# Transformer tower on one core: one softmax bound per head, auxiliary pieces on even quads, a rewritten preparation

## The reference

```python
patches = 8x8 patches of x                                  # 1024 tokens of 64 values
h = patches @ W.T + b + pos_embed                           # [1024, 64]
y = layernorm(h)
q, k, v = y@Wq + bq, y@Wk + bk, y@Wv + bv                   # 8 heads of 8
scores = q.k / sqrt(8) + col_bias[head, key]                # 1024 x 1024 per head
h = h + softmax(scores) @ v @ Wo + bo
z = layernorm(h)
h = h + z + sum over the 2 best of 8 experts of weight_e * (gelu(z@w1[e] + b1[e]) @ w2[e] + b2[e])
```

## Time and profile before

| | us |
|---|---|
| median of 3 runs | 1176.74 |
| the profiled execution | 1175.44 |
| its span, first to last instruction | 1173.6 |
| TensorE busy in it | 1105.3 (94%) |
| ScalarE busy | 1030.7 (88%) |
| VectorE busy | 671.2 (57%) |
| first to last exp of the attention stage | 56.18 to 1011.50 |

### The profile page before, as it was taken

How to read it: one execution, slowest core, us unless ns; L and a number is a source line. 1 busy time by engine, 2 the same in 40 slices (tenths; PEclk the granted TensorE clock), 3 DMA queues, 4 the chain that set the end, 5 groups by cost and what they waited for, 6 DMA issues and landing times. The chain is left out here.

```text
span 1173.6 us, 21907 instructions
## 1 busy us (share of the span) xinstructions
PE 1105.3 (94%) x7938; PEld 326.1 (28%) x7938; DVE 671.2 (57%) x1899; ACT 1030.7 (88%) x1127; POOL 131.8 (11%) x137
## 2 busy tenths in 40 slices
PE   3399999999999999999999999999999999899998
PEld 3122222222222222222222222222222222233332
DVE  9542756565656555565656565656565624367665
ACT  0199999999999999999999999999999999754553
POOL 4302201010101010101010101010101100000000
PEclk8589999999999999999999999999999999999999
DMA  2421323232323232323232323222222220022332
GB/s 52 111 74 39 85 53 82 53 83 53 83 53 84 53 83 53 83 49 87 49 88 49 86 50 73 63 68 67 62 67 55 72 61 10 16 63 66 84 75 50
DMA packets 63041, 75.93 MB, mean 65 GB/s; under 512 B 26338, under 2 KB 31458, under 8 KB 62906
## 3 DMA queue, kind: packets, MB, share of 16 engines
q1 hardware_dynamic: 60076, 73.01, 25.1%
q10 hardware_dynamic: 2350, 1.10, 0.4%
q0 software_dynamic: 480, 0.06, 0.1%
HBM read 37.54 MB, written 36.49 MB: 63 GB/s over the span
## 5 line engine op out<-in xcount | busy, mean ns | idle before, releaser
L1247 ACT ACTIVATE probs<-psum 128x1024 f32<-128x1024 f32 x1024 | 946.5, 1144 | 13.2 <-PE psum L1446 10.9
L1462 PE MATMUL psum<-probs,VA 128*32 128x512 f32 x4096 | 547.0, 606 | 5.3 <-DVE oT L1315 0.9
L1446 PE MATMUL psum<-QA,KA 54*128 54x512 bf16 x2048 | 331.7, 385 | 20.0 <-ACTq L1266 9.1
L1446 PEld LDWEIGHTS psum<-QA,KA 54*128 54x128 bf16 x2048 | 75.0, 93 | 491.5 <-ACT probs L1247 448.3
L1315 DVE STREAM_TRANSPOSE oT<-psum 128x512 f32<-128x512 f32 x64 | 45.9, 717 | 143.3 <-PE psum L1462 143.3
L1462 PEld LDWEIGHTS psum<-probs,VA 128*32 128x32 f32 x4096 | 82.1, 108 | 144.6 <-issue 86.1
L1282 ACT ACTIVATE probs<-psum,b 128x1024 f32<-128x1024 f32 x64 | 67.9, 1111 | 53.6 <-PE psum L1515 53.5
L1393 DVE TENSOR_TENSOR probs<-probs,psum 128x1024 f32<-128x1024 f32 x64 | 78.2, 1221 | 51.6 <-PE psum L1525 30.4
L484 DVE TENSOR_SCALAR qk<-psum,b_qk,scale_qk 128x512 f32<-128x512 f32 x32 | 25.8, 810 | 134.4 <-PE psum L673 134.4
L1515 PE MATMUL psum<-m_x,w 64*128 64x512 f32 x256 | 60.5, 591 | 1.5 <-ACT probs L1282 1.5
L1539 PE MATMUL psum<-probs,w 128*64 128x512 f32 x256 | 60.9, 598 | 0.0
(11 more groups left out here) (175 smaller groups left out, 830.9 us busy)
## 6 DMA issues: line engine op xcount, KB each, us to landing
QA<-q_parts_d SPq DMA_DIRECT2D x64, 192.0 KB
KA<-k_parts_d SPq DMA_DIRECT2D x64, 192.0 KB
q_parts_d<-qk_parts SPq DMA_DIRECT2D x31, 192.0 KB, 2.5
k_parts_d<-qk_parts SPq DMA_DIRECT2D x31, 192.0 KB, 2.7
xT<-in_xT SPq DMA_DIRECT2D x16, 256.0 KB, 2.6
x_d<-x2T SPq DMA_DIRECT2D x16, 256.0 KB, 2.1
m_x<-x_d SPq DMA_DIRECT2D x16, 256.0 KB, 2.7
out_h<-result SPq DMA_DIRECT2D x16, 256.0 KB, 3.2
```

Of the source, the lines that this page charges most:

```text
L1247: nc.scalar.activation(probs[:, k % PROB_BUFS, :], score_buf(buf_of(k)), ACT.Exp).then_inc(exped, 1)
L1446: last = pe.matmul(score_buf(buf_of(k))[:, (g % 2) * BANK:(g % 2 + 1) * BANK], KA[rows_of(h, SCORE_ROWS), h // 2, jt * P:(jt + 1) * P], QA ...
L1462: last = pe.matmul(o_acc[32 * g:32 * g + 32, :], VA[:, jt, h, :], probs[:, k % PROB_BUFS, (g % 2) * BANK:(g % 2 + 1) * BANK], start=(jt == ...
```

## The change

- **One bound per head.** The per-query shift goes, with `shift_of`, `sq`'s copy, the store to DRAM and its load. Instead `sq` clips the root `rq` at 32 and spreads it over a diagonal; a new piece `bound` (in place of `flag`) multiplies it with ones, so that all partitions have the 8 roots, and VectorE reduces them to `lift`, one negative bound per pair of heads. The exp takes it as its bias. The shift rows of QA are filled with zeros by `load_shift`. The column bias has its own maximum subtracted once.
- **Even quads.** The pieces get other slots, and so do scale, centre, lead, normalise, weigh and the router's exp.
- **GpSimd's order.** In an image `prep_rstd` now comes ahead of `copy_v(0)`; in the preparation `prep_rq(0)` comes ahead of `prep_rstd(1)`.
- **Preparation.** One-hots with three instructions over pairs of edges; VA zeroed by ScalarE; the fills of `ones3` and `zeros3` after the one-hots; bias rows moved from SBUF to SBUF in six transfers, three on each of two queues; the exp table used early; 8 warm-up matmuls at the end of TensorE's part; the second half of q and k parts stored by SP at the start of the attention stage.

```diff
-AUX_SLOTS = {0: ("qk0", 0), 1: ("qk0", 1), 2: ("qk1", 0), 4: ("qk1", 1), 6: ("out_proj", 0), 7: ("out_proj", 1),
-             10: ("sq", 0), 13: ("post_t", 0), 16: ("router", 0), 18: ("router", 1), 19: ("flag", 0), 20: ("v", 0),
-             21: ("v", 1), 23: ("embed", 0), 24: ("embed", 1), 26: ("combine_t", 0), 29: ("norm_t", 0)}
+AUX_SLOTS = {0: ("qk0", 0), 2: ("qk0", 1), 4: ("qk1", 0), 6: ("qk1", 1), 8: ("out_proj", 0), 10: ("out_proj", 1),
+             12: ("sq", 0), 14: ("post_t", 0), 15: ("bound", 0), 16: ("router", 0), 18: ("router", 1), 20: ("embed", 0),
+             22: ("embed", 1), 24: ("v", 0), 26: ("v", 1), 28: ("combine_t", 0), 30: ("norm_t", 0)}
-CENTRE_SLOT, SCALE_SLOT, LEAD_SLOT, NORM_SLOT = 7, 9, 25, 27
-ROUTER_EXP_BLOCK = 38
+CENTRE_SLOT, SCALE_SLOT, LEAD_SLOT, NORM_SLOT = 10, 12, 23, 26
+ROUTER_EXP_BLOCK = 40
-COMBINE_SLOT, WEIGH_SLOT = 20, 22
+COMBINE_SLOT, WEIGH_SLOT = 20, 25
-RQ_LIMIT = 31.0
+RQ_LIMIT, RQ_CLIP = 31.0, 32.0
+WARM_MATMULS = 8
...
                 elif step == "sq":
-                    v.tensor_copy(sq[:, :], bank)
                     v.reduce_max(sq_max[:, :], bank, AX.X).then_inc(free, 1)
                     v.wait_ge(free, freed)
                     alone(v)
                     square_bounds(link)
-                    shift_of(bp, link, close)
-                elif step == "flag":
-                    v.tensor_scalar(flags[0:1, ds(bp, 1)], bank[0:1, 0:1], 1.0, None,
-                                    ALU.min).then_inc(free, 1)
+                    v.wait_ge(rq_ready, bp + 1)
+                    link(v.tensor_scalar(rq_clipped[:, :], rq[:, :], RQ_CLIP, None, ALU.min))
+                    close()
+                    v.tensor_scalar(rq_diag[:, :], ident[0:H, 0:H], rq_clipped[:, 0:1], None,
+                                    ALU.mult).then_inc(rq_spread, 1)
+                elif step == "bound":
+                    v.tensor_reduce(rq_top[:, :], bank[0:1, 0:H], AX.X, ALU.max)
+                    v.tensor_reduce(lift[:, bp % 2, :], bank[:, 0:H].rearrange("p (j t) -> p j t", t=2), AX.X, ALU.max,
+                                    negate=True).then_inc(free, 1)
...
-                elif step == "flag":
-                    pe.wait_ge(excess_ready, n + 1)
+                elif step == "bound":
+                    pe.wait_ge(rq_spread, n + 1)
                     alone(pe)
-                    last = pe.matmul(aux[0:1, 0:1], excess[:, :], ones8[:, :], start=True, stop=True)
+                    last = pe.matmul(aux[:, 0:H], ones8[:, :], rq_diag[:, :], start=True, stop=True)
...
+            def place_bias(eng, par):
+                eng.wait_ge(bparts_ready, 1)
+                for a in range(PARTS):
+                    r = HALF_ROWS * par + BIAS_ROW + a
+                    eng.dma_start(KA[r:r + 1, :, :].rearrange("o h (c p) -> o (h c) p", p=P),
+                                  bparts[32 * par:32 * par + 32, a, :]).then_inc(bparts_moved, 16)
...
-                    for n in range(32):
-                        v.tensor_scalar(hot_b[:, n, :], node_bf[:, :], float(n), exp_bits[:, 0:1].bitcast(F32),
-                                        ALU.is_equal, ALU.mult)
-                    for n in range(32):
-                        last = v.tensor_scalar(hot_a[:, n, :], node_af[:, :], float(n), None, ALU.is_equal)
-                    last.then_inc(hot_ready, 1)
+                    link(v.tensor_tensor(hot_b[:, :, :, :], nodes_b, each, ALU.is_equal))
+                    v.tensor_scalar(hot_b[:, :, :, :], hot_b[:, :, :, :], exp_bits[:, 0:1].bitcast(F32), None, ALU.mult)
+                    v.tensor_tensor(hot_a[:, :, :, :], nodes_a, each, ALU.is_equal).then_inc(hot_ready, 1)
+                    v.memset(ones3[:, :], 1.0).then_inc(ones_ready, 1)
+                    v.memset(zeros3[:, :], 0.0).then_inc(ones_ready, 1)
...
+                    for n in range(WARM_MATMULS):
+                        pe.matmul(first_bank["qk1"], ident_bf[:, :],
+                                  hot_b[:, 0:8, :, :].rearrange("p m b t -> p (m b t)"), start=True, stop=True)
...
-                    nc.scalar.activation(probs[:, k % PROB_BUFS, :], score_buf(buf_of(k)),
-                                         ACT.Exp).then_inc(exped, 1)
+                    pair = 2 * (k // (BLOCKS // 2)) + k % 2
+                    nc.scalar.activation(probs[:, k % PROB_BUFS, :], score_buf(buf_of(k)), ACT.Exp,
+                                         bias=lift[:, b % 2, pair:pair + 1]).then_inc(exped, 1)
```

More of the change, by code:

```diff
@@ L122, in attention @@
 def attention(nc, pool, io, psum, scratch, out):
-    H_all, bmax, ident, ident_bf = (pool[k] for k in ("H_all", "bmax", "ident", "ident_bf"))
-    q_parts_d, k_parts_d, shift_d, fb_d = (scratch[k] for k in ("q_parts", "k_parts", "shift", "fb"))
+    H_all, ident, ident_bf = (pool[k] for k in ("H_all", "ident", "ident_bf"))
+    q_parts_d, k_parts_d, fb_d = (scratch[k] for k in ("q_parts", "k_parts", "fb"))
     x2_d, cT_d = scratch["x2"], scratch["cT"]
@@ L209, in attention @@
         rq = sb("rq", [H, 1], F32)
[L210 to L214, removed]
+        rq_clipped = sb("rq_clipped", [H, 1], F32)
+        rq_diag = sb("rq_diag", [H, H], F32)
+        rq_top = sb("rq_top", [1, 1], F32)
+        lift = sb("lift", [P, 2, H // 2], F32)
         flags = sb("flags", [1, NB], I32)
@@ L235, in attention @@
         first_bank = {step: psum[:, i * BANK:(i + 1) * BANK] for step, i in
-                      dict(embed_0=7, embed_1=6, norm_t_0=2, qk0=3, qk1=4, v=7, sq=3, norm_t_1=2, flag=6).items()}
+                      dict(embed_0=7, embed_1=6, norm_t_0=2, qk0=3, qk1=4, v=7, sq=3, norm_t_1=2, bound=6).items()}
         w_loaded = sem("w_loaded")
@@ L355, in store_combine @@
                 sp.dma_start(cT_d[bq, :, :], cT[:, :]).then_inc(cT_stored, 16)
[L357 to L363, removed]
             def load_rows(hg):
@@ L376, in load_shift @@
                     r = slice(HALF_ROWS * par + SHIFT_ROW, HALF_ROWS * par + SHIFT_ROW + PARTS)
-                    rows = shift_d.rearrange("a (h t) i -> t a h i", t=2)
-                    sp.dma_start(QA[r, pairs, :], rows[par, :, pairs, :]).then_inc(aug_loaded[hg], 16)
-            return load_x, all_parts, first_parts, store_x2, store_combine, store_shift, load_rows, load_shift
+                    zeros = zeros3[:, :].bitcast(BF16).unsqueeze(1).broadcast_to([PARTS, 2, T])
+                    sp.dma_start(QA[r, pairs, :], zeros).then_inc(aug_loaded[hg], 16)
+            return load_x, all_parts, first_parts, store_x2, store_combine, load_rows, load_shift
         def pool_steps(g):
@@ L532, in square_bounds @@
                 v.tensor_tensor(rq2[:, :], q_sq_max[:, :], k_sq_max[:, :], ALU.mult).then_inc(rq2_ready, 1)
[L533 to L553, removed]
             lead = (lead_step, lead_centre, normalise)
-            first = (spread_of, lead_subtract, split_low, square_bounds, shift_of)
+            first = (spread_of, lead_subtract, split_low)
             return chain, measure, centre, lead, prep_step, first
@@ L837, in _ @@
                         act.dma_start(w_router[t * D:(t + 1) * D, t, :], io["router_wT"]).then_inc(router_loaded, 16)
+                    act.wait_ge(const_ready, 2)
+                    nc.scalar.activation(VA[:, :, :, :].rearrange("p c h d -> p (c h d)"),
+                                         zero1[:, :].broadcast_to([P, NCH * H * 32]), ACT.Copy).then_inc(room_set, 1)
+                    nc.scalar.activation(first_exp[:, :], half[:, :], ACT.Exp).then_inc(table_loaded, 1)
+                    act.wait_ge(table_loaded, 1)
                     act.wait_ge(first_filled, FIRST_STEPS.index("norm_t_0") + 1)
                     nc.scalar.activation(xnT[:, :], first_bank["norm_t_0"], ACT.Copy).then_inc(first_turned, 1)
[L840 to L851, removed]
-                    act.wait_ge(const_ready, 2)
-                    nc.scalar.activation(first_exp[:, :], half[:, :], ACT.Exp).then_inc(table_loaded, 1)
-                    act.wait_ge(table_loaded, 1)
-                    act.wait_ge(bparts_moved, 48)
+                    place_bias(act, 1)
+                    act.wait_ge(bparts_moved, 96)
                 @block.gpsimd
```

130 lines of the change are left out of this document (72 added, 58 removed).

## The result

The changed kernel took **1244.8 us** (median of 4 runs, 1244.5 to 1245.84) against 1176.3 us of the kernel before on the same chip (4 runs, 1175.11 to 1177.24): ratio 1.058, 95% interval 1.0566 to 1.0603. It is slower by 68.5 us, where 15 were forecast. Slower was the likeliest sign of the forecast, but for another reason than the one that the runs show; the time lies 45 us above the upper end of the range.

A forecast was written before the change was run, and what follows sets the result against it. ScalarE (59.16 us) and TensorE (58.87) were both taken as full in an image of 59.55 us. +25.5 - 8.5 - 2.3 = +14.7 on 1175.44 gave 1190.1; with 1.3 for the median 1191, range 1156 to 1200.

The forecast's parts named there:

- the likeliest sign of the forecast: Whole kernel: slower was given a chance of 0.71, faster 0.26, same 0.03.
- Part 2: One bound per head, read by the exp as a bias column: taken as 0 us, bounds 0 and 13.
- Part 1: Pieces moved to even slots: TensorE waits for VectorE's drains, +1.85 us per image, +25.5 us in all (12 to 31).
- the order on VectorE: Attention slots: x2T copied out 13.2 us after slot 9's start, v drained 6.95 us after slot 25's.
- Rival (a): Attention stage: even spacing works, no piece waits, -10.6 us there and 1155 us for the whole; chance 0.20.
- Part 3: Preparation: first score at 46.8 us, -8.7 taken as -8.5 us (-4 with slow one-hots, -10 at best).
- The one-hots and the bias parts: Preparation: one-hots take 2.3, 1.2 and 2.3 us, bias parts ready at 41.4 us instead of 45.76.
- the three issues of the bias rows: Preparation: three issues on each queue take 1.2 us, followed by one landing of 2.1 us.
- the positional add's 4.64 us: Preparation: the add took 4.64 us beside GpSimd's fill of VA, where such an add takes 0.69: -3.95 us.
- Part 4: Eight warm-up matmuls before the first score: TensorE's clock may be up in image 0, -2.3 us (0 to -4).

The follow-up runs named there:

- e2: The kernel before, with only its exp taking a bias from a column of zeros written once: 1254.1 us, ratio 1.0665 to the kernel before.
- e7: e5 plus 24 more exps in ScalarE's idle preparation time, at sizes 64, 256 and 512, with and without a zero column: 1159.5 us (one run).
- e1: The changed kernel with its exp without the bias column, the bound's subtraction left out: 1186.4 us, ratio 1.0089 to the kernel before.
- e4: e1 with the old table of slots and the old slots of the other steps, bound where flag stood: 1166.99 us, ratio 0.9924.
- e3: e1 with post_t moved from slot 14 to 15, bound from 15 to 19, weigh_experts from 25 to 24: 1164.28 us, ratio 0.9904.
- e5: e3 with the router's exp after block 38 instead of 40: 1158.86 us, ratio 0.9855 to the kernel before.
- e8: e5 with the one-hots stored in the old layout, neighbours in one matmul 256 bytes apart: 1164.37 us, ratio 0.9902.
- e6: e5 with 17 warm-up matmuls instead of 8: 1158.78 us against 1158.86 of e5.
- e10: e9 with no warm-up matmuls instead of 8: 1159.46 us against 1159.29 of e9.
- e9: e5 with the bound subtracted again, by TensorE through one of QA's shift rows, the exp without a column: 1159.29 us, ratio 0.9859.

## Why the prediction was wrong, step by step

**Part 2 failed: "bounds 0 (the bias was a column before) and ... 13 us; I take 0, as the shape and engine stay."** It is +90.5 us of ScalarE's time. Three things were wrong in that sentence. The bias was no column before: the exp's row in the profile of before names `psum` alone as its source. The upper bound was miscalculated: 0.14 us on each of 1024 exps is 143 us, not 13, and with that the range would have had to be far wider. And rows near enough to give the price stood in the trace of before, unread. An exp by itself took 1.02 us; the Gelus of the same shape, with a column as bias, 1.111 on average (another function, so by themselves a hint and no proof; e2 and e7 are the proof):

```profile
56.18 1.02 ACT L1247 ACTIVATE probs<-psum 128x1024 f32<-128x1024 f32 x1 [4.37 <-PE psum L1446]
```

```profile
L1282 ACT ACTIVATE probs<-psum,b 128x1024 f32<-128x1024 f32 x64 | 67.9, 1111 | 53.6 <-PE psum L1515 53.5
```

The difference, 0.09, times 64 on an engine that has 0.8 us to spare per image, is the result: 58.7 + 5.7 = 64.4 us per image.

**With ScalarE alone the bound, the other terms of the attention stage stopped counting.** Part 1's +25.5 were waits of TensorE. In the profile after they are smaller, since TensorE itself comes later, and they cost nothing: it is busy for 60.6 us of 64.5 and they fit into the rest. Post_t no longer waits; the bound piece waits for x2T, the combine transposes for v_new:

```profile
530.88 0.35 PE L673 MATMUL psum<-rq_diag,ones 8*128 8x8 f32 x2 [0.39 <-DVE x2T L568]
...
557.08 0.40 PE L687 MATMUL psum<-ident_bf,comb_parts 128*128 128x128 bf16 x4 [0.42 <-DVE v_new L478]
```

x2T is drained at 530.73, 12.85 us after the start of slot 9 at 517.88 (forecast 13.2), and v_new at 557.02, 6.84 after that of slot 25 at 550.18 (6.95), so the order on VectorE was followed rightly. The sign of the forecast was thus right by luck: the loss that it had worked out is real in e1 and worth nothing in the kernel as changed, whose loss is the term that was put at 0. What it is worth, e1 against e4: 1.53 per image and 19.4 us, of the 1.85 and 25.5 forecast (12 to 31). Rival (a), even spacing without waits, was wrong for this table; with three steps moved (e3, e5) it comes true but for 0.4 us per image, at 1159.

**Part 3 held**: -7.7 us for -8.5. The one-hots and the bias parts came within 0.6 us of the forecast. The first score was 0.9 later than forecast: the three issues of the bias rows took 2.11 instead of 1.2, and from their end to the score are 4.8 us instead of 2.1 + 2.06 (the page has a median of 3.8 from issue to landing for these rows, where 2.1 was taken), less the 0.6 by which the bias parts were early. In the cause of one term it was wrong: the positional add's 4.64 us were put down to GpSimd's fill; e8 shows VectorE held for as long beside the strided histogram with no fill there. Which of the two held the add itself was not tried.

**Part 4, the warm-up, gave nothing**: the clock fell in the gap before the first score, as the text allowed, and none or twice as many matmuls change no time (e6, e10). Image 0 does have less stall, 3.3 us in e4 and 1.3 to 2.7 in the respaced kernels against 3.9 before; e10, without a warm-up, has 1.5, so the warm-up has no part in it. What has was not tried.

**The sum.** With ScalarE as the bound it is 1175.4 - 7.7 + 90.5 - 13.3 - 0.4 = 1244.5; the profiled execution took 1245.84, its span having 3.1 us around it instead of 1.84.

## What to carry to other kernels

Before anything is added to an instruction of the engine that sets the pace, compare operand lists, not shapes: one more operand on 1024 instructions cost ScalarE 90 us here and the kernel 58 (e1) to 78 (e2), and a row with the same operand stood in the same profile. A constant per head that an activation would add can go through a spare row of the matmul that feeds it; here that cost nothing above the spread of the runs (e9). And a bound of a cost belongs multiplied out beside its count, since an edit taken as 0 by a wrong product is never looked at again.

## What the runs showed of the hardware

- A column as the bias makes an activation dearer by 0.09 us at 64, 256, 512 (e7) and 1024 elements (e1, e2), with a column of zeros as with one of changing bounds.
- 128 matmuls of 32 columns take 1.29 us when the elements that they read lie 4 bytes apart (after, e5), and 4.6 to 4.9 us when they lie 256 bytes apart (before, e8), all at a granted clock of 1.00. While these ran in e8, VectorE started nothing for 4.13 us; the cause of that stays open.
- TensorE's clock rose for good at 54.9 us with no warm-up matmuls (e10), at 56.5 with 17 (e6) and at 54.3 to 57.9 in the kernels with 8 (e3 and e7 the ends; e8, whose scores start 6.7 us later, left out), though the first scores started at 47.3 to 48.1 in all of them, at a clock of 1.0 in e6 and of 0.50 in e5 and e10.
